# A two-layer attention and experts kernel: hand-placed work moved between units and steps, and the experts' weights awaited a group later

## What is computed

```
x = x + attention0(norm(x), ctx)     # 8 heads of 8 channels, rotary, output projection
x = x + experts0(norm(x))            # 64 experts, top 8, 256 -> 96 -> 256, silu(gate)*up
x = x + attention1(norm(x), ctx)     # 8 heads of 8 channels, no rotary
x = x + experts1(norm(x))            # 64 experts, top 8, with a capacity
```

## Time and profile before

| | us |
|---|---|
| median of 3 runs | 2177.61 (2177.58 to 2186.87) |
| the profiled execution | 2174.09 |
| its span, first to last instruction | 2172.4 |
| TensorE busy | 1717.8 (79%) |
| VectorE busy | 1454.2 (67%) |
| ScalarE busy | 1261.7 (58%) |
| GpSimd busy | 973.4 (45%) |
| mean granted TensorE clock | 0.94 of full |

### The profile page before, as it was taken

The page is one execution under the profiler, slowest core; times in us unless marked ns, Lnnn a source line. Parts: engine busy times, 40 slices in busy tenths (PEclk is TensorE's granted clock), DMA queues, the critical chain, the costliest instruction groups (busy, mean ns, idle before and its releaser), DMA issues. The chain is left out here.

```text
span 2172.4 us, 45251 instructions
## 1 busy us (share of the span) xinstructions
PE 1717.8 (79%) x12879; PEld 1131.3 (52%) x12879; DVE 1454.2 (67%) x4556; ACT 1261.7 (58%) x3268; POOL 973.4 (45%) x1114
## 2 busy tenths in 40 slices
PE   4999999898972999999995487887887778856551
PEld 2555555555542788898884134444444444534440
DVE  5888888888853445555434478988998989843331
ACT  1777776666751566666664367777776767732210
POOL 4266666666654000000003655555555554138883
PEclk9999999999995999999997599999999999968996
DMA  5678877777634976666664677886767665358856
GB/s 146 150 210 232 216 198 196 194 203 196 185 103 148 342 226 199 198 201 198 197 192 137 171 169 190 199 204 172 178 174 171 173 169 152 79 146 190 187 94 111
DMA packets 413088, 390.98 MB, mean 180 GB/s; under 512 B 46640, under 2 KB 385072, under 8 KB 412848
## 3 DMA queue, kind: packets, MB, share of 16 engines
q1 hardware_dynamic: 341888, 259.97, 45.2%
q0 software_dynamic: 37904, 90.22, 16.7%
q10 hardware_dynamic: 33056, 37.90, 6.0%
HBM read 233.74 MB, written 170.16 MB: 186 GB/s over the span
## 5 line engine op out<-in xcount | busy, mean ns | idle before, releaser
L851 ACT ACTIVATE prob<-psE 128x512 f32<-128x512 f32 x1024 | 603.2, 597 | 319.1 <-PE psE L1427 267.9
L1042 DVE TENSOR_REDUCE mx<-psS 128x2 f32<-128x512 f32 x1024 | 682.5, 674 | 121.8 <-PE psS L1416 111.4
L710 POOL DMA_INDIRECT yg<-y_d,row_all x256 | 257.6, 1006 | 646.9 <-SPq L373 486.1
L1427 PE MATMUL psE<-q,k 128*128 128x256 bf16 x2048 | 398.3, 277 | 43.7 <-ACT prob L851 37.8
L1416 PE MATMUL psS<-k,q 128*128 128x512 bf16 x1024 | 399.7, 392 | 18.6 <-DMA k<-k_stack_d 8.9
L1532 PE MATMUL psE<-wt,xgT 128*128 (+1 forms) x1536 | 325.3, 335 | 1.2 <-ACT xgT L943 1.0
L1368 DVE TENSOR_TENSOR hid<-sil,psE 128x96 f32<-128x96 f32 x384 | 97.5, 254 | 335.4 <-ACT sil L948 310.4
L698 POOL DMA_INDIRECT xs_d<-xr,posi x256 | 251.3, 982 | 127.0 <-ACT prob L851 79.2
L1427 PEld LDWEIGHTS psE<-q,k 128*128 128x128 bf16 x2048 | 182.9, 99 | 235.5 <-ACT prob L851 97.8
L1443 PE MATMUL psO<-prob,v 128*32 128x256 f32 x4096 | 278.0, 389 | 9.4 <-ACT osb L832 9.4
L943 ACT COPY xgT<-psS 128x256 f32<-128x256 f32 x384 | 144.5, 376 | 205.5 <-PE psS L1526 143.1
(11 more groups left out here) (217 smaller groups left out, 2682.8 us busy)
## 6 DMA issues: line engine op xcount, KB each, us to landing
xg<-xs_d SPq DMA_DIRECT2D x320, 128.0 KB, 2.6
y_d<-y_all SPq DMA_DIRECT2D x320, 128.0 KB, 2.4
q<-q_stack_d SPq DMA_DIRECT2D x128, 256.0 KB
k<-k_stack_d SPq DMA_DIRECT2D x128, 256.0 KB
wt<-in_gu ACTq DMA_DIRECT2D x128, 192.0 KB
q_stack_d<-parts SPq DMA_DIRECT2D x64, 192.0 KB
k_stack_d<-parts SPq DMA_DIRECT2D x64, 192.0 KB
wt<-in_dn ACTq DMA_DIRECT2D x128, 96.0 KB
```

Source lines behind the costliest of these rows:

```text
L710: g.indirect_dma_start(yg[:, k, :], None, y0_d[:, :], bass.IndirectOffsetOnAxis(row_all[:, row(st.pair("load") * K + k, 1)], 0))\
L851: a.activation(prob[gr][:, u % 4, :], psE[ring][:, :], ACT.Exp, scale=SCALE).then_inc(s_exp, 1)
L1042: v_.tensor_reduce(mx[b][:, bg // 4, :].rearrange("p (h r) -> p h r", h=2)[:, :, (bg % 4) * 2 + tt], psS[(UNITS * (st.s0 - LAG["smax"]) + ...
L1427: ins = m_.matmul(psE[ring][:, i * T:(i + 1) * T], k2[b][:, bg, hh * T + i * P:hh * T + (i + 1) * P], q2[b][:, bg, :], start=True, stop=True)
```

## The change

- Second layer, steady steps: the adds of comb go from units 4, 6, 9, 10 to 4, 5, 7, 8; the first sum from 5 to 6, the second from 8 to 7; the closing add into `x2` from unit 13 to 9; the moments of `x2` from units 0 and 1 of the next step to 10 and 11 of the same. `hotr` goes from unit 7 to unit 0, the rank cast from 10 to 13. On ScalarE the router's normalise, ScalarE's half of the one-hot, the router's copy and the first part each go one unit earlier; TensorE's router transposes go from 11 to 10. The paces of gathers 5, 6, 7 go from units 8, 10, 11 to 7, 8, 9.
- Second layer, fill: GpSimd issues gathers 0 to 4 of a pair in its step and 5 to 7 in the next step behind `roots` and ahead of `remainder`; the comb work of the first pairs goes to late units; in step 4 Q goes to unit 15 and to a bank of the exponentials.
- First layer: scatters 0 to 4 of a pair go a step earlier (stage place), 5 to 7 stay; one VectorE instruction of two is left for the places, at unit 5 instead of 8. SP reads its first table rows ahead of the barrier.
- Slots of both layers: TensorE awaits a group of weights eight slots later.

```diff
-PACE = ((0, 2, 4, 6, 8, 10, 12, 14), (2, 3, 4, 5, 6, 8, 10, 11))
+PACE = ((6, 8, 10, 12, 14, 0, 2, 4), (2, 3, 4, 5, 6, 7, 8, 9))
+AT_ONCE = 5
+FULL = 6
-ADDED = (4, 6, 9, 10)
+ADDED, TWO, ONE, ALL, MOMENTS = (4, 5, 7, 8), 6, 7, 9, (10, 11)
+def units_of_products(s0):
+    if s0 >= FULL:
+        return PRODUCTS
+    return (12, 13, 14, 15) if s0 == FULL - 2 else (8, 9, 10, 11)
+def units_of_sum(s0):
+    if s0 >= FULL:
+        return ADDED, TWO, ONE, ALL, MOMENTS
+    if s0 == FULL - 1:
+        return (10, 11, 13, 14), 12, 13, 15, (15, 15)
+    return (0,) * 4, 0, 0, 0, (0, 0)
+AHEAD_OF_ROOTS = 5
...
-                if before and s % FB == 0 and s < E:
-                    before(s // FB)
+                if before and s % FB == 0 and 0 < s <= E:
+                    before(s // FB - 1)
...
                 if L == 0:
                     clear_end(sp, mybir.EngineType.SP)
+                    sp.wait_ge(s_r3, 2)
+                    table = {}
+                    first_rows(table, 0)
                 barrier(sp, 2 + 2 * L)
...
                 def scatter(k, unit):
-                    if not st.on("post"):
+                    stage = "place" if k < AT_ONCE else "post"
+                    if not st.on(stage):
                         return
...
                 roots()
                 if L == 0:
-                    for k in (0, 1, 2, 3):
+                    for k in (5, 6, 7):
                         scatter(k, PACE[L][k])
+                    scatter(0, PACE[L][0])
                     rotated()
-                    for k in (4, 5):
+                    for k in (1, 2):
                         scatter(k, PACE[L][k])
                     remainder()
-                    scatter(6, PACE[L][6])
+                    scatter(3, PACE[L][3])
                     third_part()
-                    scatter(7, PACE[L][7])
-                elif st.on("attn"):
-                    for k in range(K):
-                        gather(k, PACE[L][k])
+                    scatter(4, PACE[L][4])
+                else:
+                    if 0 < st.s0 < FULL:
+                        for k in range(AHEAD_OF_ROOTS, K):
+                            gather(Step(1, st.s0 - 1), k, 0)
+                    if st.s0 >= FULL - 1:
+                        for k in range(K):
+                            gather(st, k, PACE[L][k])
                     remainder()
                     third_part()
-                else:
-                    remainder()
-                    third_part()
-                    for k in range(K):
-                        gather(k, PACE[L][k])
+                    if st.s0 < FULL - 1:
+                        for k in range(AHEAD_OF_ROOTS):
+                            gather(st, k, 0)
...
-                    if L == 1 and u == 11 and st.on("post"):
+                    if L == 1 and u == 10 and st.on("post"):
                         act.wait_ge(s_eq, st.n1("post"))
...
-                    if u == (10, 12)[L] and st.on("route"):
+                    if u == (10, 11)[L] and st.on("route"):
                         act.wait_ge(s_xtp, st.n("route"))
...
-                    if u == (6, 9)[L] and st.on("route"):
+                    if u == (6, 8)[L] and st.on("route"):
...
-                    if u == 11 - L and st.on("front"):
+                    if u == (15 if filled else (11, 9)[L]) and st.on("front"):
...
+                    if L == 1 and st.s0 >= FULL - 1:
+                        sums(st, u)
+                    if L == 1 and st.s0 < FULL - 2 - 1 and u == 15:
+                        sums(st, 0)
+                    if L == 1 and st.s0 == FULL - 2 and u == 7:
+                        sums(Step(1, FULL - 3), 0)
+                    if L == 1 and st.s0 == FULL - 2 and u == 15:
+                        sums(st, 0)
...
-                    if u == 7 and st.on("post") and L == 1:
+                    if u == 0 and st.on("post") and L == 1:
+                        ch.join("rankf")
+                        wait(dve, s_lsp, st.n1("post", 1, 0))
                         v_.tensor_tensor(hotr[:, :, :], over_k(iota_r), over_e(rankf[:, 0, :], P), ALU.is_equal)\
                           .then_inc(s_lhs, 1)
...
-                    if L == 1 and u == 0 and st.on("front"):
-                        dve.wait_ge(s_x2, st.n1("front"))
-                        ch.add(v_.bn_stats(stats[:, 0, :], x2[st.buf("front")][:, :]), "stats0")
...
-                    if u == 10 + L and st.on("route"):
+                    if u == 10 and st.on("route"):
```

More of the change, by code:

```diff
@@ L458, in nbuf0, with slots @@
                 return self.it * 16 + 16 * ((self.s0 - FLAG[stage]) // FB + 1 - back)
[L460 removed]
+        def slots(layer, body, look_up=None, before=None, aside=None, table=None):
             end = JOBS[layer] + FLAG["D"]
[L463 removed]
+            table = {} if table is None else table
             for s in range(end):
```

137 lines of the change are left out of this document (81 added, 56 removed).

## The result

The changed kernel takes 2169.57 us (median of 20 runs, 2157.32 to 2189.97) where the kernel before takes 2181.91 (20 runs beside it): a ratio of 0.9951, 95% interval 0.9932 to 0.9970. By that ratio it is 10.7 us faster, by the two medians 12.3; the forecast was 27.5. The longest of the 20 runs is a slow one and does not enter the ratio. The profiled executions say the same: span 2160.8 us against 2172.4.

A forecast was written before the change was run, and what follows sets the result against it. It took VectorE's queue and TensorE's chain to bound the second layer's steady steps, the largest piece, and GpSimd's rounds the fill. Terms summed to -27.5 us: 2146.6 for the profiled execution, median 2150, 8-in-10 range 2128 to 2174.

The forecast's parts named there:

- A: First layer's scatters: five fewer behind the last pair, at 1.26 us each; -6.3 us, bounds -4 and -6.3.
- B: First slots: X of tile 0 waits only for group 0's weights and its tile; -5.0 us, bounds -2.6 and -6.4.
- C: Second layer's fill: GpSimd's rounds 15 us instead of 18, gathers filling a wait; -7.5 us, bounds -3 and -11.
- rival 4: Fill or first slots do nothing (step 5 stalls or tiles come late): C -3 or B -2.6, median 2155 to 2160; 14%.
- D: Second layer's 31 steady steps: less VectorE work, closing add 992 to 416 ns; -0.3 us a step, -9, bounds +19 and -26.
- rival 1: Steady steps: `nrm` later, Q some 9.0 us behind first reduction; D +19, median 2178 (7%), or +62, 2222 (5%).
- E: Last pairs: the last LIST waits for `hotr`, `hote` and ScalarE's half in a row; +0.6 us, bounds 0 and +1.2.
- F: Second layer's slots: TensorE starts behind weights though its first tile has landed; -0.3 us, bounds 0 and -1.

The follow-up runs named there:

- m2_sum: The changed kernel with the third pair's sums in the second layer's fill moved to the end of step 3, ahead of step 4's first eight reductions: 2074.69 us, ratio 0.9859.
- e2_weights: The kernel before with only one part of the change, each group of eight experts' weights awaited eight slots later: 2102.23 us, ratio 0.9997 to the kernel before.
- after_again: The changed kernel unaltered, run again beside the kernel before in a faster group: 2082.65 us, ratio 0.9896.
- e8_early_copies: The changed kernel with 20 added DRAM-to-DRAM copies of 192 KB, issued by GpSimd at every second slot from the fourth: 2087.86 us, ratio 0.9921 to the kernel before.

## Why the prediction was wrong, by its own steps

- **A** (-6.3): the tail measured -6.3 in every trace of the new order. What it left out is a price of the new order in the first layer's steps, which it put at 0 give or take 3: 2.6 to 5.9 us in the faster groups, against one trace of the old order. In the traces of the first measurement no such price shows (-2.8).
- **B** (-5.0, bounds -2.6 and -6.4): measured -0.6, and -0.5 to -1.2 alone. This is the first step that failed. It named one thing that X would wait for, its tile, and priced that well (3.25 us behind the barrier, forecast about 4). It did not ask what is queued on ScalarE ahead of tile 0's copy: 18 issues, 8.5 us, hidden before by the wait for weights that the change removes. And behind that gate lies a second that it named and did not price: full DMA engines.
- **C** (-7.5, bounds -3 and -11): measured +1.6. This is the second step that failed. The round of 15 us came, twice; the third round did not: the step followed GpSimd's list but did not ask where the sums that gather 4 waits for stand on VectorE. It saw the stall of step 5 and not that of step 4. Against the fill it replaced the new one is worth nothing to the second pair, and m2_sum shows the cause by taking it away: one sum placed earlier gives 7.0 us. That is rival 4's case, beyond its figure of -3, and by another wait than the one rival 4 names.
- **D** (-0.3 a step): median -0.29, as worked out: the closing add from 992 to 418 ns, half of it lost elsewhere in the step. First to last exponential gave 6.9 us, not 9. `nrm` at 8.99 us is just outside the 8.2 to 8.9 named and Q starts 9.1 us in, the sign of rival 1; its price did not come. The reading beneath was incomplete: the middle wait of 1.71 us was taken for the length of TensorE's chain, and for the most part it is the lateness of TensorE's signals; where they are not late the wait is 0.14 us before and 0.55 after, and D is -0.7 a step. So that the figure came out in the first traces is in part luck.
- **E, F**: +1.1 us in the last two stretches together, within what two executions differ.
- **The total**: -27.5, and then 4.4 missing in B, 9.1 in C (+1.6 for -7.5), 2.1 in D and 0.8 in E and F, with -0.6 in the stretches it put at 0: -11.7, the measured -11.6 but for rounding. B and C at the weak ends of their bounds were -5.6 together; they measured +1.0. Rival 4 took one or the other to fail; its own terms give 2152 for B, 2155 for C and 2157 for both, not the 2155 to 2160 that it states.

## What to carry to other kernels

When a wait is removed, list what stands in every engine's queue between the old and the new release, DMA issues included, and then check whether the DMA engines have a share to spare: where they are full, an earlier start buys nothing. In a pipeline's fill follow each semaphore to the place of its setter in the other engine's list, since one sum placed behind eight reductions held three queues. Before pricing a wait for matmuls, compare the end of their row with the start of the reader: where the two lie microseconds apart, the wait is not the length of the chain of rows, and a sum made from those lengths misprices it.

## What the runs showed of the hardware

- The same program, the kernel before, takes 2102 to 2103 us in three groups of runs and 2174 to 2182 in three others, at a mean granted clock of 0.94 in both; two groups under one chip number, 7, differ in this way. From first to last exponential the first layer takes 553 us in a faster group (e2_weights, whose steps there are the same) and 587 in the first trace, the second layer's steps behind the fourth pair 569 to 570 and 604.5. In the slower groups TensorE's semaphores come up to 2.9 us behind the modelled ends of its matmuls in mid-step; in the faster ones they follow at once, and steps repeat to 0.02 us. The cause is not known.
- A VectorE instruction that met GpSimd's remainder in these rows ended with it or up to 0.3 us behind it, whatever its own length: an add of 0.42 us takes 1.50, a cast of 128x16 values 1.43 instead of 0.15. The Trainium skill, page SBUF — State Buffer, section SBUF: two separate sides, says that the loser of the shared port pair blocks for the whole instruction. The traces agree in that. By the page the one that starts first has the pair; here VectorE's instruction starts first, by 0.04 and 0.23 us, and is the one that waits (the profile's spans on GpSimd are rough). The page names two SBUF inputs or a two-port mode as the condition, and the cast has one input, so it would have to be such a mode, which no run here shows.
- Full DMA engines (share 1.05 to 1.07) moved 336 to 350 GB/s in windows of 20 us, and 373 with copies from DRAM to DRAM added (after, after_again, e8_early_copies).
